# Level tables of a language-model tower: the one-hots made from a broadcast read instead of matmuls

## The reference

```python
# part 1: nesting level of each token, clipped to 0..31, and its embedding
lvl = clip(lvl + is_open - is_close, 0, 31)      # scan along the 256 tokens of a row
h   = level_emb[levels] * 0.15                   # 32 levels x 256 features
# part 2: attention with relative positions, 16 heads of 16, on layernorm(h)
scores = (Q K^T + Q Er[rel]^T) / 4
h = h + softmax(scores) V Wo^T
# part 3: rmsnorm, full attention, top-2 of 8 experts, on layernorm(h)
h = h + ffn(layernorm(h))
```

## Time and profile before

| | |
|---|---|
| median of 3 runs | 795.88 us |
| the profiled execution, its own time | 796.95 us |
| its span | 795.1 us |
| PE busy in the span | 747.8 us (94%) |
| DVE, ACT, POOL busy | 464.6, 372.8, 187.8 us |
| tables block, to the first matmul of the first attention | 31.07 us |
| head of the first attention, to the first maximum | 31.07 to 38.59 us |

### The profile page before, as it was taken

How to read it: one execution, slowest core, us unless ns; L and a number is a source line. 1 busy time by engine, 2 the same in 40 slices (tenths; PEclk the granted TensorE clock), 3 DMA queues, 4 the chain that set the end, 5 groups by cost and what they waited for, 6 DMA issues and landing times. The chain is left out here.

```text
span 795.1 us, 19240 instructions
## 1 busy us (share of the span) xinstructions
PE 747.8 (94%) x7245; PEld 563.5 (71%) x7246; DVE 464.6 (58%) x1113; ACT 372.8 (47%) x616; POOL 187.8 (24%) x292
## 2 busy tenths in 40 slices
PE   3899999999999998999998989999999999999994
PEld 1377777777767886455545754555799999999993
DVE  7777777767636555999964874711344444444441
ACT  4677777777633443476773323210333333333330
POOL 5400000000003443333320230165222323223232
PEclk8599999999999999999999999999999999999998
DMA  5400000000011346444466900022523233232331
GB/s 166 171 2 2 2 3 2 3 2 2 3 48 41 107 133 173 124 127 123 121 229 205 318 0 17 13 88 80 167 40 53 47 46 53 40 53 47 46 47 20
DMA packets 70545, 58.97 MB, mean 74 GB/s; under 512 B 7553, under 2 KB 62153, under 8 KB 70481
## 3 DMA queue, kind: packets, MB, share of 16 engines
q1 hardware_dynamic: 62048, 47.61, 19.6%
q0 software_dynamic: 7152, 9.38, 7.2%
q10 hardware_dynamic: 1280, 1.08, 0.4%
HBM read 35.02 MB, written 22.95 MB: 73 GB/s over the span
## 5 line engine op out<-in xcount | busy, mean ns | idle before, releaser
L1474 POOL DMA_INDIRECT out<-ex_Y,ex_to x39 | 60.6, 1553 | 166.1 <-DVE ex_Y L1749 163.0
L652 ACT ACTIVATE la_PT<-ps 128x512 f32<-128x512 f32 x128 | 69.5, 594 | 46.5 <-PE ps L553 46.1
L1214 DVE TENSOR_REDUCE fa_m<-ps 128x2 bf16<-128x512 f32 x128 | 84.2, 682 | 6.7 <-PE ps L1083 5.5
L1703 DVE TENSOR_TENSOR ex_hT<-ps,ex_sl 128x512 f32<-128x512 f32 x39 | 27.0, 691 | 99.0 <-PE ps L1540 99.0
L1184 ACT ACTIVATE fa_PT<-ps 128x1024 f32<-128x1024 f32 x64 | 65.5, 1024 | 39.5 <-PE ps L1098 39.0
L1547 PE MATMUL ps<-WD,ex_hT 128*128 x312 | 74.0, 380 | 1.6 <-DVE ex_Y L1749 0.8
L1540 PEld LDWEIGHTS ps<-ex_xT,V 128*128 128x128 f32 x640 | 74.5, 192 | 1.2 <-ACT ex_xT L1593 0.2
L1540 PE MATMUL ps<-ex_xT,V 128*128 128x128 f32 x640 | 74.8, 275 | 0.0
L1540 PEld LDWEIGHTS ps<-ex_xT,XS 128*128 128x128 f32 x608 | 70.8, 192 | 0.9
L1540 PE MATMUL ps<-ex_xT,XS 128*128 128x128 f32 x608 | 71.0, 275 | 0.0
L671 DVE TENSOR_TENSOR la_SM<-ps,la_SA 128x512 bf16<-128x512 f32 x64 | 44.3, 692 | 38.1 <-ACT la_SA L634 19.5
(11 more groups left out here) (263 smaller groups left out, 1438.3 us busy)
## 6 DMA issues: line engine op xcount, KB each, us to landing
QK<-qk_parts SPq DMA_DIRECT2D x192, 64.0 KB, 2.3
qk_parts<-pj_parts SPq DMA_DIRECT2D x16, 384.0 KB, 2.8
expert_in<-zfill SPq DMA_DIRECT2D x1, 5070.0 KB, 16.1
ex_XR<-expert_in SPq DMA_DIRECT2D x39, 130.0 KB, 2.0
WG<-in_e_gate SPq DMA_DIRECT2D x8, 512.0 KB, 6.9
WU<-in_e_up SPq DMA_DIRECT2D x8, 512.0 KB, 10.7
WD<-in_e_down SPq DMA_DIRECT2D x8, 512.0 KB, 9.9
out<-HS SPq DMA_DIRECT2D x4, 512.0 KB, 5.5
```

Source lines behind the costliest of these rows:

```text
L652: nc.scalar.activation(PT[:, n // 2 % 2, jh, n % 2], ps[:, 2 * (n % 2) + jh], ACT.Exp, scale=QK_SCALE).then_inc(s_exp[jh], 1)
L1214: nc.vector.reduce_max(m[:, b % 2, grp, 2 * k:2 * k + 2], ps[:, h % 2].rearrange("p (f j) -> p f j", f=2), AX.X).then_inc(s_max, 1)
L1474: nc.gpsimd.indirect_dma_start(out=outs, out_offset=bass.IndirectOffsetOnAxis(ap=to[:, n:n + 1], axis=0), in_=Y[:, n], in_offset=None, com ...
```

## The change

1. The matmuls that spread the levels (L395, L405), the tile `lev4` (L332), the selection matrices and ScalarE's one-hots (L252, L254) are gone.
2. SP stores `t_lev` to a DRAM tensor `levels` of 2048 bf16, waits for it, and reads it back twice, each time 1024 values (a "quad" of 4 rows) broadcast to the 128 partitions of `LEVB`.
3. VectorE compares `LEVB` in SBUF with the partition's number, 1024 columns at a time: 4 instructions for a quad of `OHX` and one for `OH3`. Quad 0 stands at the end of the tables block, quad 1 in the first attention, between the sixth unit's copy and the first maximum.
4. `OHX` has the heads outside of the tokens now, so the matmuls of the units write PSUM in steps of four elements.
5. The parts of Q and K are written where they are used (`QKT`): VectorE writes four of twelve slots by its casts, ScalarE copies the others. GpSimd does the same for `EP`, and its `zfill` memset comes first.
6. identB and negIB are made by ScalarE; VectorE's first token instructions come ahead of `t_xt`; `OHT` comes ahead of `ac`. TensorE gets 2, 3 and 9 spin matmuls in the tables block.
7. The store of `zfill` waits for the first half of `LEVB` too.

```diff
+def one_hot(nc, g, quad):
+    V = nc.vector
+    for h in range(HG):
+        last = V.tensor_scalar(g.OHX[:, quad, h].rearrange("p b i -> p (b i)"), g.LEVB[:, quad], g.code[:, h:h + 1], None, ALU.is_equal)
+    last.then_inc(g.s_oh, 1)
+    V.tensor_scalar(g.OH3[:, quad * BP * S:(quad + 1) * BP * S], g.LEVB[0:L3, quad], g.lvl[:, 0:1], None, ALU.is_equal).then_inc(g.s_oh, 1)
...
+                sp.wait_ge(s_lv, 1)
+                sp.dma_start(g.lv.rearrange("o (b s) -> (o b) s", b=B), lev[:]).then_inc(s_lvd, 16)
+                sp.wait_ge(s_lvd, 16)
+                for q in range(NQUAD):
+                    sp.dma_start(g.LEVB[:, q], g.lv[:, q * BP * S:(q + 1) * BP * S].to_broadcast([P, BP * S])).then_inc(s_lvb[q], 16)
+                sp.wait_ge(s_lvb[0], 16)
                 sp.wait_ge(s_made, 2)
...
-                def one_hot(x):
-                    act.wait_ge(s_ohb[1], x + 1)
-                    nc.scalar.activation(sq[:, x % 2], ps[:, 2 + x % 2], ACT.Square, bias=code[:, 1:2]).then_inc(s_sq, 1)
...
+                for src, k, at in ((0, 0, slice(1, 4, 2)), (0, 1, slice(2, 6, 2)), (5, 0, slice(2, 3)), (5, 1, slice(1, 2))):
+                    act.wait_ge(s_part, 1 if src == 0 else 2)
+                    n = len(range(SLOTS)[at])
+                    copy(slots[:, k, :, at], slots[:, k, :, src].unsqueeze(2).to_broadcast([P, NG, n, DK])).then_inc(s_keep, 1)
...
-                V.scalar_tensor_tensor(lev4[:], lev[:].unsqueeze(2).to_broadcast([B, S, HG]), float(HG), h4[:].unsqueeze(1).to_broadcast([B, S, HG]),
-                                       ALU.mult, ALU.add).then_inc(s_lv, 1)
...
-                for n in range(SLOTS):
-                    at = slice(n * DK, (n + 1) * DK)
-                    do(V.tensor_copy(g.QT[:, :, at], parts[LEFT[n]][:, 0]))
-                    do(V.tensor_copy(KT[:, :, at], parts[RIGHT[n]][:, 1]))
...
+                dve.wait_ge(s_lvb[0], 16)
+                one_hot(nc, g, 0)
...
@@ level_attention
-                    rhs = g.OHX[:, quad * BP:(quad + 1) * BP, i0:i0 + CH, :]
+                    rhs = g.OHX[:, quad, :, :, i0:i0 + CH]
+                    def spread(bank, n):
+                        return ps[0:n, bank].rearrange("p (b i h) -> p h b i", b=BP, h=HG)
...
                 for u in range(FIRST):
                     keep_unit(u)
+                for q in range(1, NQUAD):
+                    dve.wait_ge(g.s_lvb[q], 16)
+                    one_hot(nc, g, q)
                 halves_max(0)
```

More of the change, by code:

```diff
@@ L180, in tables @@
     s_in = [sem("in_" + n) for n in ("tok", "tab", "w", "er", "id", "wo", "bias", "dump", "const")]
-    s_ohb, s_ohx = ([sem("tab_" + n + k) for k in names(2)] for n in ("codes", "onehot"))
     s_dve, s_pool = sem("tab_dve"), sem("tab_pool")
-    s_lv, s_lvp, s_oh, s_sq, s_ln, s_keep, s_proj, s_sp, s_turn, s_qkTc, s_ac, s_made, s_idb, s_rs = (
-        sem("tab_" + n) for n in "levels levelsB onehot3 square norm kept proj split turned qkTc ac made idb rstd".split())
+    s_lv, s_lvd, s_ln, s_keep, s_proj, s_part, s_sp, s_turn, s_qkTc, s_ac, s_made, s_idb, s_rs = (
+        sem("tab_" + n) for n in "levels stored norm kept proj part split turned qkTc ac made idb rstd".split())
+    s_lvb = g.s_lvb = [sem("tab_spread" + n) for n in names(NQUAD)]
+    g.s_oh = sem("tab_onehot")
     with ExitStack() as c:
@@ L189, in tables @@
         acc, Dl, nD, rD, zer = (sb(n, [B, S], F32) for n in ("acc", "Dl", "nD", "rD", "zer"))
[L190 to L193, removed]
+        lev, iotaL = sb("lev", [B, S], BF16), sb("iotaL", [P, L], F32)
         emb, xt, bo = sb("emb", [L, D], F32), sb("xt", [L, D], F32), sb("bo", [L, D], F32)
@@ L274, in _ @@
                 do(G.memset(half[:], -0.5))
-                do(G.memset(one[:], 1.0))
+                do(G.memset(zfill, 0.0))
                 pool.wait_ge(s_ln, 1)
@@ L282, in _ @@
                 pool.wait_ge(s_in[3], 16)
-                split(G, do, er[:], e1[:], e2[:], [x[:] for x in eparts])
-                for n in range(SLOTS):
-                    do(G.tensor_copy(EP[:, :, n], eparts[RIGHT[n]][:]))
-                G.memset(half[:], -0.5).then_inc(s_made, 1)
-                do(G.memset(zfill, 0.0))
+                split(G, do, er[:], e1[:], e2[:], [EP[:, :, n] for n in (0, 5, 3)])
+                do(G.tensor_copy(EP[:, :, 2:6:2], EP[:, :, 0].unsqueeze(2).to_broadcast([P, 4, 2, DK])))
+                G.tensor_copy(EP[:, :, 1], EP[:, :, 5]).then_inc(s_made, 1)
                 pool.wait_ge(s_in[7], 16)
@@ L338, in _ @@
                     do(V.tensor_tensor(tab[:, n].rearrange("p g d -> p (g d)"), ps[:, 5 + n, 0:NG * DK], bias[:, n].rearrange("p g d -> p (g d)"), ALU.add))
-                split(V, do, tab[:], r1[:], r2[:], [x[:] for x in parts])
-                for n in range(SLOTS):
-                    at = slice(n * DK, (n + 1) * DK)
-                    do(V.tensor_copy(g.QT[:, :, at], parts[LEFT[n]][:, 0]))
-                    do(V.tensor_copy(KT[:, :, at], parts[RIGHT[n]][:, 1]))
+                do(V.tensor_copy(slots[:, :, :, 0], tab[:]), s_part)
+                do(V.tensor_tensor(r1[:], tab[:], slots[:, :, :, 0], ALU.subtract))
+                do(V.tensor_copy(slots[:, :, :, 5], r1[:]), s_part)
+                do(V.tensor_tensor(r2[:], r1[:], slots[:, :, :, 5], ALU.subtract))
+                for k, n in enumerate((4, 3)):
+                    V.tensor_copy(slots[:, k, :, n], r2[:, k]).then_inc(s_part, 1)
                 dve.wait_ge(s_proj, 4)
@@ L347, in _ @@
                                 ALU.add).then_inc(s_sp, 1)
[L349 to L358, removed]
+                dve.wait_ge(s_turn, 1)
+                V.tensor_copy(qkT[:, 1].rearrange("p h l -> p (h l)"), ps[0:KP, 6].bitcast(BF16)[:, 0:512]).then_inc(s_qkTc, 1)
+                dve.wait_ge(s_in[8], 48)
                 dve.wait_ge(s_ac, 1)
[L360 to L362 removed]
                 do(V.tensor_tensor(g.OHT[:].rearrange("p j b l -> p (j b) l"), iotaL[:].unsqueeze(1).to_broadcast([P, 2 * B, L]),
                                    levT.unsqueeze(2).to_broadcast([P, 2 * B, L]), ALU.is_equal))
[L365 to L366 removed]
+                dve.wait_ge(s_ac, 2)
+                do(V.tensor_copy(ac[:], ps[:, 0, 0:NG * L].rearrange("p (g l) -> p g l", g=NG)))
+                split(V, do, ac[:], a1[:], a2[:], [g.ACP[:, :, n * L:(n + 1) * L] for n in range(3)])
+                dve.wait_ge(s_lvb[0], 16)
+                one_hot(nc, g, 0)
+                dve.wait_ge(s_sp, 1)
+                dve.wait_ge(g.s_oh, 2)
             @block.tensor
@@ L388, in _ @@
                 last.then_inc(s_proj, 1)
[L390 to L406, removed]
@@ L420, in _ @@
-                last.then_inc(s_turn, 1)
-                codes(1, 4)
-                pe.wait_ge(s_sp, 1)
-                for n, t in enumerate((g.QT, KT)):
-                    for k in range(NG):
-                        last = nc.tensor.transpose(ps[0:KP, 5 + n].bitcast(BF16)[:, k * P:(k + 1) * P], t[:, k], g.identB[:])
-                last.then_inc(s_turn, 1)
-                codes(1, 5)
-                for q in range(2, 4):
-                    levels(q)
-                for x in range(2):
-                    codes(0, x)
@@ L432, in _ @@
-                pe.wait_ge(s_qkTc, 2)
-                for h in range(H):
-                    last = mm(ps[(h % HG) * L:(h % HG + 1) * L, 7, (h // HG) * L:(h // HG + 1) * L], qkT[:, 0, h], qkT[:, 1, h], start=True, stop=True,
-                              skip_group_check=True)
-                last.then_inc(s_ac, 1)
-                pe.wait_ge(s_keep, 3)
+                pe.wait_ge(s_idb, 2)
+                spin(nc, g, 2, 2)
+                pe.wait_ge(s_lv, 1)
                 for j in range(2):
@@ L440, in _ @@
                 last.then_inc(s_ac, 1)
-                for x in range(2, CUT):
-                    codes(1, x + 4)
-                    codes(0, x)
+                spin(nc, g, 2, 3)
+                pe.wait_ge(s_part, 4)
+                pe.wait_ge(s_keep, 5)
+                for n in range(2):
+                    for k in range(NG):
+                        last = nc.tensor.transpose(ps[0:KP, 5 + n].bitcast(BF16)[:, k * P:(k + 1) * P], g.QKT[:, n, k], g.identB[:])
+                last.then_inc(s_turn, 1)
+                pe.wait_ge(s_made, 1)
+                for n in range(4):
+                    last = nc.tensor.transpose(ps[0:KP, 3].bitcast(BF16)[:, n * P:(n + 1) * P], EP[:, n].rearrange("p s d -> p (s d)"), g.identB[:])
+                last.then_inc(s_turn, 1)
+                pe.wait_ge(s_qkTc, 2)
+                for h in range(H):
+                    last = mm(ps[(h % HG) * L:(h % HG + 1) * L, 0, (h // HG) * L:(h // HG + 1) * L], qkT[:, 0, h], qkT[:, 1, h], start=True, stop=True,
+                              skip_group_check=True)
+                last.then_inc(s_ac, 1)
+                spin(nc, g, 2, 9)
 def level_attention(nc, g):
```

75 lines of the change are left out of this document (24 added, 51 removed).

## The result

The changed kernel takes 811.83 us, the median of 4 runs (809.99 to 812.89), where the kernel before took 795.74 beside it. The ratio is 1.0195, with a 95% interval of 1.0183 to 1.0207: 16 us slower. The forecast was 791.7 us, in a range of 784.2 to 793.8. It was wrong; what happened is rival 4, which had 0.04.

What follows compares the result with a forecast made beforehand. TensorE was taken to bound the long stretch of the first attention, not the tables block or head ahead. 796.95 - 10.5 + 5.1 + 1.2 = 792.75 us, less 1.07 for the profiled execution: 791.7 us, range 784.2 to 793.8.

Steps and rivals of the forecast that it cites:

- rival 4: Units inside the steps: TensorE writes single elements in steps of four at half speed, 24.7 us more, 816 us; chance 0.04.
- Strided writes of TensorE: Units' matmuls: writing PSUM in single elements in steps of four was taken to cost nothing.
- Tables block: Block before the first attention: its successor starts at 20.6 instead of 31.07 us, a gain of 10.5 us.
- The compares: End of tables block: five VectorE compares of 1024 bf16 columns at 0.43 us each, 2.15 us.
- collisions: Tables block: GpSimd's embedding chain delays six or seven VectorE instructions by 0.2 us each, 1.1 us.
- The spread: Tables block: store and reads of the levels by DMA stay hidden, with 1 to 2.5 us of slack.
- landings: Tables block: the levels' DMA store lands 2.0 to 2.8 us after issue, the read of quad 0 the same.
- Memsets: Head of first attention: quad 1's compares wait for GpSimd's memsets, so the first maximum starts later, a loss of 5.1 us.
- Clock: First attention: TensorE idles in the head, its clock falls, and the low clock afterwards loses 1.2 us (0 to 2.5).
- the failed step: Units' matmuls: the assumption that single-element PSUM writes in steps of four cost nothing.
- the wait: Head of first attention: compares held by GpSimd's memsets delay the first maximum, 5.1 us.

Runs made afterwards that it cites:

- e9: Kernel before, with the units' matmuls writing PSUM in runs of four elements, 64 bytes from run to run: 797.22 us.
- e4: Kernel before, with the units' matmuls writing PSUM in steps of four elements (single f32, 16 bytes apart): 818.08 us.
- e7: Kernel before, with the units' matmuls writing PSUM in steps of two elements (single f32, 8 bytes apart): 816.63 us.
- e3: Changed kernel, with GpSimd's three memsets of QK waiting for quad 1's compares: 805.08 us.
- e1: Changed kernel, but the units write PSUM in a row and VectorE's and ScalarE's copies out of PSUM turn the order: 792.99 us.
- e2: Changed kernel, but TensorE reads its moving operand in the old order (steps of 2 KB) and writes PSUM in a row: 861.39 us.
- e5: Changed kernel with the edits of both e1 and e3: 784.49 us.
- e6: e5 with quad 1's five compares moved back into the tables block, behind quad 0's: 787.71 us.
- e11: Kernel before, with the units' moving operand read in steps of two bf16 (4 bytes), PSUM written in a row: 796.09 us.
- e10: Kernel before, with the units' moving operand read in steps of four bf16 (8 bytes), PSUM written in a row: 819.02 us.

## Why the prediction was wrong

- The wrong step is "Strided writes of TensorE": "I take single elements in steps of four at nothing". They cost 0.17 us more for L479 and 0.22 for L482 than L518 and L521 took. The L539 that I leaned on the earlier trace rows writes runs of four, and e9 shows that such runs are free; singles are not (e4, e7). The row bore out a form that the change doesn't have. I had the other end as rival 4 with its price (24.7 us, from 0.213 more for each matmul; measured 18.4 in the steps, 0.17 and 0.15 us a matmul: before, the matmul behind L521 started 0.28 us behind it on average and not 0.21, so part of the second one's price was there already) and the point from which it decides, and gave it 0.04. A price in a stretch of 189 us that TensorE bounds at 98% asked for more than one nearby row.
- Tables block: right in kind, 11.7 us for 10.5. The compares cost 0.41 us for 0.43, from the last compare's end to the first unit 0.61 us for 0.5, collisions less than half of the 1.1 us. The spread was hidden, as said: quad 0's compares began 0.03 us behind VectorE's own list. The earlier trace rows give landings of 2.3 and 2.8 us, and the 2.0 that I began from isn't there; SP issued the two reads 1.2 us behind the store (10.01 and 11.25 us), and they took 3.1 and 3.3 us to land, which the slack covered.
- Memsets: right in kind, and near in size (5.1 us forecast, 4.5 measured, and e3 takes it away). The step from a CAST that was 0.18 us late to a memset of 3.5 us held. The Trainium skill's rule of the exclusive pair ("SBUF — State Buffer", "Who interferes with whom") is borne out by the 1.66 and 3.81 us.
- Clock: right that it falls, but it cost 2.6 us where the sum had 1.2 (the 7.50 us between the first maximum and the second step's unit against 4.86 in e3), just above the 2.5 that I had as its high end.
- Without the failed step the sum nearly stands: e1, which mends it alone, runs at 792.99 us, and the forecast was 791.7. Its terms miss in both directions, though, so that some of this is luck. By e1's rows the tables block gives 10.8 us (10.5 forecast), the wait costs 4.5 (5.1), the low clock 2.5 (1.2), and 0.6 us more lie behind it.

## What to carry to other kernels

When the layout of an operand changes, someone has to turn the order, and the price depends on who does it: 19 to 22 us if TensorE writes single f32 elements in steps, 68 if it reads single bf16 values far apart (e2 against e1), nothing for the copies that carry PSUM away anyway. A row bears out a stride only if it has the same run length: pairs in PSUM and a step of two bf16 in SBUF were free, single f32 and a step of four bf16 were not. And a fast VectorE instruction in SBUF may stand next to a long GpSimd memset only if nobody waits for it; one wait on GpSimd gave back 6.7 us of the changed kernel, and 8.5 with the writes mended (e5 against e1).

## What the runs showed of the hardware

- A matmul of 512 columns takes 0.22 us when PSUM is written in pairs or longer runs, and 0.39 to 0.43 when single f32 elements are written 8 or 16 bytes apart; the factor is about the same at the low clock (granted 0.50): 0.77 us from L479 to L482 at 35.09 us in the changed kernel, and 0.43 from L478 to L481 at 22.17 in e6.
- Reading its moving operand in bf16, it takes 0.23 us in steps of 4 bytes, 0.43 in steps of 8 bytes and 0.84 in steps of 2 KB (e11, e10, e2).
- VectorE and ScalarE read PSUM with the head taken from 512 bytes apart at the price of a row: 684 and 592 ns (e1), 685 and 592 before.
- A memset by GpSimd on one partition of 4096 elements, 3.51 us, holds off a compare of VectorE in SBUF until it ends (1.66 and 3.81 us for a compare that takes 0.48), while casts out of PSUM beside it keep their 0.69 us.
